# A pipelined four-layer graph network kernel: products with their high parts first, loop waits one group ahead, a new beginning and end

## The chip, the cores and the metric

One core of one Trainium2 chip. The metric is the device time of one execution in microseconds. The core's engines are TensorE (PE, matmuls and transposes), VectorE (DVE), ScalarE (ACT), GpSimd (POOL) and the queue of SyncE (SP), which issues every DMA.

## The reference

128 graphs of 128 nodes, 256 features each. x goes through four layers, each followed by a residual and a layer norm; adj is a sparse weighted 128x128 matrix per graph. Cut to what is computed (norm is a layer norm without gain, H = (adj != 0)):

```
h  = layernorm(relu(D^-1 H B^-1 H^T (x W1^T) + b1)) * gamma + beta     # 512 features
x1 = norm(2 x + D^-1 H B^-1 H^T (h W2^T) + b2)                          # layer 0
x2 = norm(x1 + relu([x1, adj x1 / rowsum(adj)] W^T))                    # layer 1
x3 = norm(x2 + adj(relu(adj(relu(adj(x2 V1)+b1) V2)+b2) V3)+b3)         # layer 2
x4 = norm(x3 + relu((adj x3) Wk) * any(x3 != 0))                        # layer 3
```

## The kernel before, in words

**The unit of work is a pair of graphs** (g = 0, 1); there are 64 pairs. Each pair passes through a chain of stages on TensorE, named in the code: G (the matrix of H B^-1 H^T), Tr (its transpose, after VectorE scaled it into Gd), Gx (G times the input), R (times W1), P (times W2) with squares (the sums for the layer norm of h), GP (G times P), xT (transpose of x1), XAB, AXB (layer 1), Ax2, H1, H1W, H2, H2W, AP3 (layer 2), Ax3, TK (layer 3). Between two stages ScalarE and VectorE, or GpSimd, take the result out of a bank of PSUM.

**fp32 by parts.** A product of two full-precision matrices is made of three passes in fp32r: each operand is held as a high part (rounded by a ScalarE copy, `high_...` or `round_...`) and a low part (the difference, `low_...` on VectorE or GpSimd); the passes are high x high, high x low, low x high. `product` (lines 377 to 382) issues the three of each term together. Before it, a stage waits for the high part and the low part of what it multiplies. Stages named propagate_T (Gx, Ax2, H2, Ax3) and the transposes (Tr, xT) use plain fp32 operands: eight 128x128 products, or two or four transposes.

**A software pipeline written out by hand.** Every engine has its own list of calls: `fill()`, then `body(n)` for n = 7 to 61 (FIRST to LAST - 1), then `drain()`. body(n) works on pairs n+1 to n-5 at once: G, Tr and Gx of pair n, R, P and GP of n-1, XAB and AXB of n-2, Ax2 to H2 of n-3, H2W to TK of n-4, norm n4 of n-5. The order within a queue is the order of the calls; queues meet only in semaphores (wait_ge). fill and drain are orders of their own, over 100 calls on most engines. The eight PSUM banks are given by BANK in the loop and by BANK_OF for stages in fill and drain. Because a bank is used again by another stage, TensorE's lists also have bare waits such as `pe.wait_ge(gt_hi, n)`: the reader of the old contents must be done. They may stand several calls ahead of the stage that writes the bank.

**The loop around the change.** On TensorE (lines 735 to 774) the order is R, G, xT, H2W, Ax2, XAB, H1, AP3, P, squares, Tr, AXB, H1W, Ax3, Gx, H2, GP, TK. Tr waits for gd_made (VectorE's Gd), Gx for gt_made (ScalarE's copy_GT of Tr's result) and for the input. On ScalarE (lines 1335 to 1370) square_mean waits for squares, VectorE turns its result into h_veps (wide_var), root_h takes the square root, make_x3 applies norm n3 (two activations of line 961, the second signals n3.done, for which Ax3 waits), then come round_p, copy_GT, copy_h1w, high_ax3, round_GT, high_gx. On GpSimd (lines 2199 to 2216) make_xb is followed by low_p (needs round_p), low_GT (needs round_GT), make_x2c, low_h2. SP reloads the inputs (a ring of four pairs) and stores x4.

Of the kernel before, what the change touches and what calls it, by code (L numbers as in the profile page):

```python
# [16 lines left out]
BANK = dict(R0=1, R1=0, Ax2=0, Tr=0, GP=4, H1=1, Gx=1, XAB=2, AXB=2, TK=2, H2=3, xT=4, P=4,  # L17
# [30 lines left out]
def build(nc, x, adjT, w1T, w2T, wab, v1, v2, v3, wk, columns, rows, eye, out):  # L48
    NP, C, GP_, D = x.shape
# [4 lines left out]
    with ExitStack() as ctx:  # L54
# [316 lines left out]
        def _(pe):  # L371
# [51 lines left out]
            def R(p, h):  # L423
                if p == 0:
                    pe.wait_ge(w1_lo, h + 1)
# [7 lines left out]
            def P(p, h):  # L433
                if p == 0 and h == 0:
                    pe.wait_ge(w2c_lo, 1)
# [1863 lines left out]
```

## Time and profile before

| | us |
|---|---|
| three runs | 1405.39, 1405.96, 1407.59 (median 1405.96) |
| the profiled execution, its own time | 1406.28 |
| its span in the profile | 1404.5 |
| TensorE matmul busy | 1378.7 (98%), 10896 instructions |
| TensorE weight loads busy | 1336.8 (95%) |
| VectorE, ScalarE, GpSimd busy | 1135.4 (81%), 1126.3 (80%), 1013.2 (72%) |
| DMA | 47.17 MB, mean 34 GB/s |

How to read it: matmuls are pipelined, each record of a matmul (0.28 us for 256 columns) overlaps its neighbours, which start about 0.12 us apart. So a hole of less than about 0.15 us between two starts doesn't show as idle time, and one looks at the starts. On ScalarE and VectorE, too, the next instruction starts before the record of the last one ends.

### The profile page before, as it was taken

How to read it: one execution, taken by the hardware profiler on the slowest of the kernel's cores; microseconds unless marked ns; L12 is line 12 of the kernel's file. 1: busy time of each engine (PE TensorE's matmuls, PEld its weight loads, DVE VectorE, ACT ScalarE, POOL GpSimd, SP SyncE). 2: the span in 40 equal slices, each digit the busy share in tenths (PEclk: the TensorE clock that was granted, in tenths of full speed). 3: DMA queues.
4: the chain of work that ended last, by engine and by line, in shares of the span. 5: the costliest groups of instructions: out<-in, count | busy, mean ns of one | idle time of the engine just before them, and what ended most of it. 6: DMA issues, size and time to landing. Idle time of an engine off the chain costs nothing. (4 is left out here: it accounts for less than half of the span.)

```text
span 1404.5 us, 35429 instructions
## 1 busy us (share of the span) xinstructions
PE 1378.7 (98%) x10896; PEld 1336.8 (95%) x10896; DVE 1135.4 (81%) x4086; ACT 1126.3 (80%) x2639; POOL 1013.2 (72%) x1065
## 2 busy tenths in 40 slices
PE   7999999999999999999999999999999999999995
PEld 7999999999999999999999999999999999999995
DVE  7888888787887887787887888877878877878886
ACT  6777887887887878878878878778878788788775
POOL 5857778777777787787787787777777877877530
PEclk9999999999999999999999999999999999999998
DMA  4100110101101101101101101011011011010001
GB/s 141 35 21 20 39 36 24 39 30 30 39 20 39 39 21 39 39 20 39 39 20 39 38 21 39 28 32 39 20 39 39 20 39 39 20 39 28 1 16 38
DMA packets 29961, 47.17 MB, mean 34 GB/s; under 512 B 3408, under 2 KB 12240, under 8 KB 29776
## 3 DMA queue, kind: packets, MB, share of 16 engines
q1 hardware_dynamic: 29776, 44.91, 10.1%
q8 instruction: 90, 1.47, 0.4%
q14 instruction: 95, 0.78, 0.2%
HBM read 28.12 MB, written 16.78 MB: 32 GB/s over the span
## 5 line engine op out<-in xcount | busy, mean ns | idle before, releaser
L961 ACT ACTIVATE x<-n_s,n_shift,n_rstd 128x256 f32<-128x256 f32 x384 | 208.4, 591 | 6.5 <-DVE n_shift L1550 5.1
L216 POOL TENSOR_TENSOR r_lo<-r_f,r_hi 128x512 fp32r<-128x512 f32 x122 | 157.7, 1293 | 45.3 <-ACT r_hi L942 40.1
L209 POOL TENSOR_TENSOR h_lo<-h_f,h_hi 128x512 fp32r<-128x512 f32 x122 | 158.1, 1296 | 40.3 <-ACT h_hi L942 40.1
L2111 POOL TENSOR_TENSOR n_s<-tk,mask 128x512 f32<-128x512 f32 x60 | 62.5, 1042 | 141.8 <-DVE mask L1603 135.1
L375 PE MATMUL psum<-v_hi,h_hi 128*128 128x256 f32 x512 | 149.6, 292 | 1.2 <-ACT tk L1123 1.0
L375 PE MATMUL psum<-w2c_hi,r_hi 128*128 128x258 f32 x512 | 145.8, 285 | 0.2 <-issue 0.2
L375 PE MATMUL psum<-w2c_lo,r_hi 128*128 128x258 f32 x512 | 144.5, 282 | 0.0
L375 PE MATMUL psum<-v_hi,h_lo 128*128 128x256 f32 x512 | 144.4, 282 | 0.0
L375 PE MATMUL psum<-gx_hi,w1T_hi 128*128 128x256 f32 x512 | 144.3, 282 | 0.1
L375 PE MATMUL psum<-v_lo,h_hi 128*128 128x256 f32 x512 | 144.1, 282 | 0.0
L1526 DVE BATCH_NORM_STATS2 n_st<-n_s 128x6 f32<-128x256 f32 x384 | 142.1, 412 | 2.2
L375 PE MATMUL psum<-gx_lo,w1T_hi 128*128 128x256 f32 x512 | 143.8, 281 | 0.0
L375 PE MATMUL psum<-gx_hi,w1T_lo 128*128 128x256 f32 x512 | 143.8, 281 | 0.0
L375 PE MATMUL psum<-w2c_hi,r_lo 128*128 128x258 f32 x512 | 143.8, 281 | 0.0
L375 PE MATMUL psum<-A_f,x 128*128 128x128 f32 x1024 | 136.2, 276 | 6.5 <-ACT x L961 6.1
L966 ACT ACTIVATE h_f<-psum,columns 128x256 f32<-128x256 f32 x256 | 107.6, 471 | 34.9 <-PE psum L375 34.6
L375 PEld LDWEIGHTS psum<-A_f,x 128*128 128x128 f32 x1024 | 125.5, 192 | 7.9 <-issue 7.8
L956 ACT ACTIVATE n_std<-psum,eps_c 128x2 f32<-128x2 f32 x165 | 42.3, 257 | 93.6 <-DVE psum L1535 93.6
L209 POOL TENSOR_TENSOR p_lo<-p_f,p_hi 128x512 fp32r<-128x512 f32 x61 | 78.1, 1280 | 51.5 <-ACT p_hi L942 51.5
L209 DVE TENSOR_TENSOR ax_lo<-psum,ax_hi 128x512 fp32r<-128x512 f32 x128 | 88.4, 691 | 26.8 <-ACT ax_hi L942 23.3
L375 PE MATMUL psum<-wab_hi,x1T_hi 128*128 128x512 f32 x256 | 106.5, 416 | 0.0
L966 ACT ACTIVATE r_f<-psum,columns 128x256 f32<-128x256 f32 x256 | 100.5, 468 | 2.2 <-PE psum L375 2.1
(166 smaller groups left out, 5379.8 us busy)
## 6 DMA issues: line engine op xcount, KB each, us to landing
x_in<-x_in_dram SPq DMA_DIRECT2D x64, 256.0 KB, 2.8
out<-x SPq DMA_DIRECT2D x64, 256.0 KB, 2.0
at_in<-adjT SPq DMA_DIRECT2D x64, 128.0 KB, 2.2
x<-v_in SPq DMA_DIRECT2D x3, 256.0 KB, 5.6
n_s<-w2T_in SPq DMA_DIRECT2D x2, 256.0 KB, 3.5
r_f<-w1T_in SPq DMA_DIRECT2D x2, 256.0 KB, 5.5
h_f<-wab_in SPq DMA_DIRECT2D x2, 256.0 KB, 5.9
tk<-wk_in SPq DMA_DIRECT2D x1, 256.0 KB, 5.5
```

Source lines behind the costliest of these rows:

```text
L209: return e.tensor_tensor(dst[1][:], src, f(dst[0][:]), ALU.subtract).then_inc(signal, 1)
L216: e.tensor_tensor(r_s[1][:, half], r_f[:, half], f(r_s[0][:, half]), ALU.subtract).then_inc(r_lo[h], 1)
L375: return pe.matmul(o, a, b, start=start, stop=stop)
L956: act.activation(nm.std[:], nm.mv(p)[:, :, 1], ACT.Sqrt, bias=eps_c[:, 0:1]).then_inc(nm.rooted, 1)
L961: last = act.activation(dst[:, g, :], nm.s[:, g, :], ACT.Identity, scale=nm.rstd[:, g:g + 1], bias=nm.shift[:, g:g + 1])
L966: return act.activation(dst[:, m].rearrange("p g c -> p (g c)"), psum[:, bank(stage, p), (m % 2) * 2 * C:(m % 2 + 1) * 2 * C], ACT.Relu, b ...
L1526: last = dve.bn_stats(nm.st[:, g, :], sum_in_psum(p, g) if nm is n1 else nm.s[:, g, :])
L2111: pool.tensor_tensor(n4.s[:], tk[:], bc(mask[:], [C, 2, D], 2), ALU.mult).then_inc(tk_masked, 1)
```

## The change

1. `product` is replaced by `early` (for each term high x high and the pass that takes the high part of the operand that comes last from the other engines, called state) and `late` (the pass with its low part). R, GP, H1, H1W, H2W, AP3 and TK issue early of the first half, wait for the low part, then late of it, then early and late of the second half; XAB, P and AXB issue early of both halves, wait, then late of both. Before early only the high part is waited for.
2. In the loop: on TensorE the waits of Tr (gd_made) and the bank wait ax2_lo stand ahead of squares; those of Gx (gt_made, x_loaded) with the two bank waits that stood between Ax3 and Gx ahead of Ax3; a wait for gx_lo stands ahead of R(n-1,0), the one for h2_relu ahead of R(n-1,1), the one for gt_hi ahead of H2. H2 writes bank 0 and not 3. ScalarE calls copy_GT ahead of root_h and round_GT ahead of make_x3. GpSimd calls low_GT ahead of low_p.
3. fill() and drain() of all engines have another order, with other engines for some of the low parts and sums, and another BANK_OF.
4. Each norm has a pad of its own for the memset ahead of bn_aggr.

The helpers and two of the stages (R stands for GP, H1, H1W, H2W, AP3 and TK; P for XAB and AXB):

```diff
-            def product(o, terms, start=True, stop=True):
-                for t, (a, b) in enumerate(terms):
+            def early(o, terms, state, start=True):
+                for t, ab in enumerate(terms):
+                    a, b = ab
                     mm(o, a[0], b[0], start and t == 0, False)
-                    mm(o, a[0], b[1], False, False)
-                    last = mm(o, a[1], b[0], False, stop and t == len(terms) - 1)
+                    mm(o, a[1 - state], b[state], False, False)
+
+            def late(o, terms, state, stop=True):
+                for t, ab in enumerate(terms):
+                    a, b = ab
+                    last = mm(o, a[state], b[1 - state], False, stop and t == len(terms) - 1)
                 return last
...
             def R(p, h):
...
                 pe.wait_ge(gx_hi, upto(p))
-                pe.wait_ge(gx_lo, upto(p))
...
+                for j, (o, terms) in enumerate(outs):
+                    early(o, terms, 0)
+                    if j == 0:
+                        pe.wait_ge(gx_lo, upto(p))
+                    last = late(o, terms, 0)
                 last.then_inc(pe_did[f"R{h}"], 1)
...
             def P(p, h):
...
+                pe.wait_ge(r_hi[h], upto(p))
+                for o, terms in outs:
+                    early(o, terms, 1, start=h == 0)
                 pe.wait_ge(r_lo[h], upto(p))
...
+                for o, terms in outs:
+                    late(o, terms, 1, stop=h == 1)
```

TensorE's loop:

```diff
             def body(n):
+                pe.wait_ge(gx_lo, n)
                 R(n - 1, 0)
-                pe.wait_ge(gt_hi, n)
+                pe.wait_ge(h2_relu, n - 3)
                 R(n - 1, 1)
...
                 pe.wait_ge(tk_relu, n - 4)
-                pe.wait_ge(h2_relu, n - 3)
                 XAB(n - 2)
...
                 P(n - 1, 0)
                 P(n - 1, 1)
+                pe.wait_ge(ax2_lo, n - 2)
+                pe.wait_ge(gd_made, upto(n))
                 squares(n - 1)
-                pe.wait_ge(ax2_lo, n - 2)
-                Tr(n)
+                Tr(n, waited=True)
                 AXB(n - 2)
                 pe.wait_ge(h2w_lo, n - 3)
                 H1W(n - 3)
-                Ax3(n - 4)
                 pe.wait_ge(h1_relu, n - 2)
                 pe.wait_ge(n4.shifted, n - 4)
-                Gx(n)
-                pe.wait_ge(n2.summed, n - 1)
+                pe.wait_ge(gt_made, upto(n))
+                pe.wait_ge(x_loaded[n % RING], inputs(n))
+                Ax3(n - 4)
+                Gx(n, waited=True)
+                pe.wait_ge(gt_hi, n + 1)
                 H2(n - 3)
```

ScalarE's and GpSimd's loop:

```diff
                 square_mean(n - 1)
+                copy_GT(n)
                 root_h(n - 1)
+                round_GT(n)
                 make_x3(n - 4)
                 round_p(n - 1)
-                copy_GT(n)
                 copy_h1w(n - 3)
                 high_ax3(n - 4)
-                round_GT(n)
                 high_gx(n)
...
                 make_xb(pool, n - 1)
+                low_GT(n)
                 low_p(pool, n - 1)
-                low_GT(n)
                 make_x2c(n - 3)
```

The beginning, cut to SP's loads (256 KB each, but 128 KB for at, 64 for the identity and 8 for the columns). Besides them, ScalarE's list now begins round_weights(0), round_inverse(0), copy_A(0), round_w1(0), round_weights(1), round_inverse(1), copy_GT(0) and has round_w1(1) four calls later (before: copy_A(0), round_weights(0), round_inverse(0), round_w1(0), round_inverse(1), round_weights(1), round_w1(1), copy_A(1), copy_GT(0)); GpSimd's begins split_weights(0), spread_high(0), spread_low(0) (before: spread_high(0), split_weights(0), spread_low(0)).

```diff
                 sp.dma_start(columns_s[:], columns).then_inc(columns_loaded, 16)
+                load_w2(1)
                 load_at(1)
-                load_w2(1)
                 load_w2(0)
+                sp.dma_start(ident[:], eye).then_inc(eye_loaded, 16)
+                load_w1(0)
                 load_at(2)
-                load_w1(0)
+                load_v(1)
                 load_x(0)
+                load_wab(0)
+                load_at(3)
+                load_w1(1)
                 load_v(2)
-                load_w1(1)
-                sp.dma_start(ident[:], eye).then_inc(eye_loaded, 16)
+                load_wab(1)
                 load_v(0)
...
```

The end. TensorE's drain before began with the waits for h1w_out, n2.shifted and p_made, then G(62), R(61,0), R(61,1), H2W(58); now R(61,0) is first, then come those for h1w_out and n2.shifted, G(62), H2W(58), R(61,1). Its last stages were AXB(63), H1(62), Ax3(60), H2W(61), H1W(62), Ax2(63), H2(62), AP3(61), TK(60), H1(63), H2W(62), Ax3(61), H1W(63), AP3(62), H2(63), TK(61), H2W(63), Ax3(62), AP3(63), TK(62), Ax3(63), TK(63). They are now AXB(63), Ax3(60), Ax2(62), AP3(61), H1(62), TK(60), H1W(62), Ax2(63), H2(62), Ax3(61), H1(63), H2W(62), TK(61), H1W(63), AP3(62), H2(63), H2W(63), Ax3(62), AP3(63), TK(62), Ax3(63), TK(63). sum_n4 of pairs 60 and 61 is called on GpSimd, of 58 on VectorE (before: the other way round), and low_h1(61) and low_h2(59) are now VectorE's.

## Rows read from the trace of the kernel before

**Rows 1.** Stretch, length, busy us of PE, PEld, DVE, ACT, POOL; PEclk, DMA share, GB/s.

```profile
0.00:124.00 124.00, 114.39 (x854) 107.70 (x855) 101.68 (x337) 89.20 (x213) 80.43 (x96) 1.00 0.18 58
124.00:1281.00 1157.00, 1156.89 (x9220) 1126.44 (x9219) 936.19 (x3414) 948.96 (x2226) 883.88 (x922) 1.00 0.11 33
1281.00:1404.50 123.50, 107.42 (x826) 102.64 (x824) 97.54 (x337) 88.10 (x202) 48.91 (x48) 0.95 0.05 18
```

**Rows 2.** The same view, of two stretches of the end.

```profile
1360.00:1380.00 20.00, 18.40 (x150) 17.60 (x149) 17.92 (x62) 16.70 (x37) 4.73 (x4) 1.00 0.04 15
1390.00:1404.50 14.50, 4.62 (x20) 4.09 (x20) 4.67 (x21) 5.19 (x11) 0.00 (x0) 0.56 0.10 36
```

**Rows 3.** Timeline of TensorE, one pass of the loop: start, us, instruction, [idle before].

```profile
700.33 0.60 PE L461 MATMUL psum<-ident,x 128*128 128x128 f32 x4
700.68 0.37 PE L375 MATMUL psum<-v_hi,h_hi 128*128 128x256 f32 x1
...
702.20 1.06 PE L375 MATMUL psum<-A_f,x 128*128 128x128 f32 x8
...
711.29 0.41 PE L415 MATMUL psum<-ident,Gd 128*128 128x128 f32 x2
711.46 0.36 PE L375 MATMUL psum<-xbw_hi,A_hi 128*128 128x258 f32 x1
...
713.70 1.05 PE L375 MATMUL psum<-A_f,x 128*128 128x128 f32 x8
714.59 1.10 PE L375 MATMUL psum<-GT,x_in 128*128 128x128 f32 x8
715.53 1.06 PE L375 MATMUL psum<-A_f,h1w 128*128 128x128 f32 x8
...
721.72 0.49 PE L461 MATMUL psum<-ident,x 128*128 128x128 f32 x3
721.97 0.37 PE L375 MATMUL psum<-v_hi,h_hi 128*128 128x256 f32 x1
```

**Rows 4.** Timeline of ScalarE in the same pass.

```profile
712.06 0.20 ACT L1046 ACTIVATE h_std<-h_veps 128x2 f32<-128x2 f32 x1 [0.43 <-DVE h_veps L1653]
712.21 1.09 ACT L961 ACTIVATE x<-n_s,n_shift,n_rstd 128x256 f32<-128x256 f32 x2
...
713.95 0.36 ACT L942 ACTIVATE GT<-psum 128x256 f32<-128x256 f32 x1
714.21 0.59 ACT L942 ACTIVATE h1w<-psum 128x512 f32<-128x512 f32 x1
```

**Rows 5.** Timeline of ScalarE, from the beginning of the kernel.

```profile
25.87 0.20 ACT L1046 ACTIVATE h_std<-h_veps 128x2 f32<-128x2 f32 x1
25.98 0.62 ACT L942 ACTIVATE r_hi<-r_f 128x512 fp32r<-128x512 f32 x1
```

**Rows 6.** Timeline of TensorE, end of the kernel.

```profile
1295.28 0.48 PE L375 MATMUL psum<-BH,HT 128*128 128x258 f32 x2 [0.83 <-issue]
...
1391.30 1.72 PE L375 MATMUL psum<-A_f,x 128*128 128x128 f32 x8 [3.23 <-ACT x L961]
1394.52 0.55 PE L375 MATMUL psum<-wk_hi,ax_hi 128*128 128x256 f32 x1 [1.50 <-DVE ax_lo L209]
```

**Rows 7.** Timeline of ScalarE, end of the kernel.

```profile
1390.06 1.09 ACT L961 ACTIVATE x<-n_s,n_shift,n_rstd 128x256 f32<-128x256 f32 x2 [0.87 <-DVE n_shift L1550]
1393.05 0.60 ACT L942 ACTIVATE ax_hi<-psum 128x512 fp32r<-128x512 f32 x1 [1.90 <-PE psum L375]
```

**Rows 8.** Timeline of TensorE, beginning of the kernel.

```profile
6.14 0.80 PE L375 MATMUL psum<-BH,HT 128*128 128x258 f32 x2 [6.14 <-POOL BH L2089]
...
116.32 0.91 PE L375 MATMUL psum<-A_f,x 128*128 128x128 f32 x6 [1.24 <-ACT x L961]
```

**Rows 9.** Timeline of GpSimd in the pass of rows 3.

```profile
714.12 1.28 POOL L209 TENSOR_TENSOR p_lo<-p_f,p_hi 128x512 fp32r<-128x512 f32 x1 [0.46 <-ACT p_hi L942]
715.80 0.73 POOL L209 TENSOR_TENSOR GT_lo<-GT,GT_hi 128x256 fp32r<-128x256 f32 x1 [0.40 <-issue]
```

More of the change, by code:

```diff
@@ L448, in GP @@
             def GP(p):
+                outs = [(psum[:, bank("GP", p), g * D:(g + 1) * D],
+                         [(part(GT_s[p % 2], ALL, g), part(p_s, ALL, g))]) for g in range(2)]
                 pe.wait_ge(p_hi, upto(p))
-                pe.wait_ge(p_lo, upto(p))
                 pe.wait_ge(gt_lo, upto(p))
-                for g in range(2):
-                    last = product(psum[:, bank("GP", p), g * D:(g + 1) * D],
-                                   [(part(GT_s[p % 2], ALL, g), part(p_s, ALL, g))])
+                for j, (o, terms) in enumerate(outs):
+                    early(o, terms, 0)
+                    if j == 0:
+                        pe.wait_ge(p_lo, upto(p))
+                    last = late(o, terms, 0)
                 last.then_inc(pe_did["GP"], 1)
@@ L490, in H1 @@
             def H1(p):
[L491 to L492 removed]
                 if p == 0:
                     pe.wait_ge(v_lo, 1)
[L495 to L497 removed]
+                outs = [(psum[:, bank("H1", p), m * 2 * C:(m + 1) * 2 * C],
+                         [(part(v_s[0], ALL, kk, cols(m)), part(ax2, ALL, kk)) for kk in range(KD)])
+                        for m in range(KD)]
+                pe.wait_ge(ax2_hi, upto(p))
+                for j, (o, terms) in enumerate(outs):
+                    early(o, terms, 0)
+                    if j == 0:
+                        pe.wait_ge(ax2_lo, upto(p))
+                    last = late(o, terms, 0)
                 last.then_inc(pe_did["H1"], 1)
@@ L502, in H1W @@
                     pe.wait_ge(v_lo, 2)
+                outs = by_state("H1W", p, h1_s, v_s[1])
                 pe.wait_ge(h1_hi, upto(p))
-                pe.wait_ge(h1_lo, upto(p))
-                weigh("H1W", p, h1_s, v_s[1])
+                for j, (o, terms) in enumerate(outs):
+                    early(o, terms, 1)
+                    if j == 0:
+                        pe.wait_ge(h1_lo, upto(p))
+                    last = late(o, terms, 1)
+                last.then_inc(pe_did["H1W"], 1)
             def H2(p):
@@ L650, in fill @@
                 XAB(2)
-                pe.wait_ge(h2_relu, 1)
-                H2W(0)
-                pe.wait_ge(h1_relu, 2)
+                pe.wait_ge(r_relu[1], 5)
+                AP3(0)
+                pe.wait_ge(h2w_lo, 1)
                 H1W(1)
@@ L728, in fill @@
                 Gx(6)
-                pe.wait_ge(n2.summed, 5)
+                pe.wait_ge(gt_hi, 7)
                 H2(3)
@@ L856, in drain @@
-                pe.wait_ge(n3.summed, 60)
-                AXB(61)
-                pe.wait_ge(n1.done, 63)
                 TK(58)
                 pe.wait_ge(xbw_lo, 62)
-                H2(60)
+                P(63, 0)
+                pe.wait_ge(n3.summed, 60)
+                H1W(60)
+                P(63, 1)
+                pe.wait_ge(h1_relu, 61)
+                H2(60)
+                pe.wait_ge(tk_relu, 59)
+                Ax2(61)
+                pe.wait_ge(n2.summed, 62)
+                Ax3(59)
@@ L1240, in fill @@
+                high_gx(4)
+                copy_h1w(0)
+                root(n2, 1)
+                round_GT(4)
+                square_mean(3)
+                make_x2(1)
+                relu_h2(0)
+                root_h(3)
+                round_h2(0)
+                root(n1, 2)
+                round_p(3)
                 relu_r(4, 0)
-                relu_h1(0)
-                round_GT(4)
-                round_h1(0)
+                high_x1T(2)
+                high_ax2(1)
                 relu_r(4, 1)
-                root(n2, 1)
@@ L1433, in drain @@
-                root_h(63)
+                relu_h1(60)
+                round_h1(60)
+                make_x4(57)
+                relu_tk(58)
+                round_r(63, 1)
+                copy_A(62)
+                root(n1, 62)
+                root(n2, 61)
+                root(n3, 59)
                 copy_h1w(60)
-                round_p(63)
-                high_x1T(62)
-                relu_tk(58)
+                make_x2(61)
+                make_x3(59)
                 relu_h2(60)
```

1168 lines of the change are left out of this document (609 added, 559 removed), and 39 rows, old and new, of the table BANK_OF.

## The prediction

> **What bounds the kernel now.** I read the busy time by stretch first. TensorE is the bound: it idles 9.61 us of the first 124 (6.14 of them ahead of its first product [rows 8], 3.47 after), 0.11 of the 1157 us of the loop, and 16.08 of the last 123.5; VectorE is at 81% in the loop, and nearly saturated (17.92 of 20) in the stretch from 1360 [rows 1, 2]. So time can come out of the loop only where TensorE's own stream has holes too small to count as idle. They show in the starts of one pass of the loop [rows 3]. A pass is 21.29 us (700.68 to 721.97). Eight plain fp32 products with more of their kind behind take 0.89 us (Ax3, 713.70 to 714.59), but Gx, eight of the same size with H2 behind, takes 0.94 (to 715.53): a hole of 0.05. xT's four transposes take 0.35 and its last three 0.25 (721.72 to 721.97), so one takes 0.10 to 0.11, and Tr, two of them, should cost 0.35 - 0.21 = 0.14; Tr takes 0.17: 0.03. Nothing else in a pass is open to this change.
>
> **The loop, part by part.** There are 55 passes (7 to 61). (a) Gx's hole is a late release: ScalarE has written GT at 714.31 (713.95 + 0.36), and Gx begins 0.28 later, at 714.59 [rows 3, 4]. The change puts the copy of GT ahead of root_h, at about 711.7 where Tr ends, so GT is there 2 us before it is needed, and Gx follows Ax3 without a wait of its own: -0.05 a pass, -2.8 us. (b) The waits for Tr move ahead of squares, all on things long done: at best -0.03 a pass, -1.7 us; at worst nothing, if the 0.03 is the price of switching to transposes. (c) What pays: round_GT now stands between root_h and make_x3. On ScalarE root_h begins 712.06 and make_x3 712.21, and x3 is written at 713.30 (1.09 later); Ax3 begins at 713.70, so there are 0.40 us between [rows 3, 4]. A copy of GT's size lets the next one start after 0.26 (713.95 to 714.21) [rows 4]; a square root of this size lets a copy start after 0.11 [rows 5]. The new order is 0.11 + 0.27 in place of 0.15: x3 comes 0.23 later, and 0.17 are left. The first GT copy costs root_h nothing: it can begin at Tr's end, 711.7, frees the engine at about 712.0, and root_h waits for VectorE until 712.06 anyway. How much must be between? Where x3 is the only thing missing and two waits stand ahead of the group, it is 0.15 (x of pair 63 is written at 1391.15, Ax3 begins 1391.30) [rows 6, 7]. Where four waits are gathered ahead of a group it was 0.28 (Gx, above). The change gathers five ahead of Ax3: h1_relu, n4.shifted, gt_made, x_loaded and n3.done. So Ax3 is between 0.02 too early and 0.11 too late; I take 0.05 late, just under the middle of the two. That eats all of (a). It eats (b) too: x3's chain starts at squares, ahead of Tr, so a faster Tr only reaches Ax3's wait sooner. Everything behind Ax3 (Gx, H2, GP, TK, the next pass) follows it unchanged. **Loop: 0.0 us, between -4.4 (neither is eaten) and +3.3** (0.06 a pass).
>
> The Trainium skill weighs in here on both sides. Perfetto Trace Analysis, section Identifying Dependency Chains, says that an instruction that waits for several engines may get EventSemaphore instructions ahead of it for the further conditions. By that rule x3's wait turns from one on the weight load into one of its own; the 0.28 against 0.15 agrees. TensorE: Matmul & The Clock Gate, section Architectural detail, gives TensorE a queue of 64 in which weight loads are pulled ahead; by that alone earlier waits would free the loads, and the loop would give the whole -4.4.
>
> (d) The passes within a product change order: all with the high part first, then a wait for the low part on the rest. Their number does not change. In the loop no product waits for a low part (0.11 us idle), so 0. Should a wait inside a product hold up the next load, 12 such waits a pass at 0 to 0.03 (Tr's hole, the nearest row to such a price) would cost 0 to 0.36 a pass. H2W, which begins behind four waits, needs 1.52 for its 12 passes with the switch from xT in them, 0.12 and a bit each, with no such hole [rows 3]; so I take 0; the upper end, +20 us, gets a chance of 0.02, outside the range. (e) H2 goes from bank 3 to bank 0, behind gt_hi, which at 712.06 + 0.11 + 0.36 = 712.5 is early enough for 715.5. On GpSimd low_GT now runs ahead of low_p: 0.73 us of work, 0.46 of it in the time in which low_p was waited for [rows 9], so p_lo ends 0.27 later, at 715.67. GP stands behind H2's eight products (from 715.53, some 0.8 us) and needs p_lo only for its third pass: 0. A later x3 also pushes copy_h1w and the next ScalarE work by under 0.1, as the copy of GT that stood there is gone: 0. (f) The separate pads of the memsets: 0. SP's order in the loop is unchanged.
>
> **The beginning.** The same work in another order of all queues, SP's loads too. 3.47 us can be had after the first product; the largest piece is 1.24 us, Ax3(2) waiting for x [rows 8]. I see two gains worked out of the order: split_weights(0) leaves the way of the first product (about 0.15), and copy_GT(0) is no longer behind copy_A(1) and the round of w1's second half, which lets Gx(0) start some 0.3 earlier. w1's second half lands later (448 KB more are ahead of it) but is needed only by R(0,1). Of the rest, low parts that arrive late are now hidden under up to four passes (0.47). I take -1.3, bounds -3.5 and +1.2 (another wait like the 1.24).
>
> **The end.** (1) G(62) stood 0.83 idle [rows 6] on n2.shifted; now R(61,0), 12 passes, is ahead of that wait: -0.8. (2) From H1(63) on, one chain sets the end. A product starts now 0.15 after the high part and not after the low part. TK(63) has its high part at 1393.65 and starts at 1394.52, 0.87 later [rows 6, 7]; 0.72 of that can go, as far as passes are there to fill it. TK has four, at half the clock 0.24 each: 0.7. H2W(63) has four at 0.12: 0.5. AP3(63) has two: 0.2. Sum 1.4; H1 and H1W of pair 63 may give as much again, but VectorE, 90% busy there [rows 2], takes that back in part: 0.4. (3) sum_n4 of pairs 60 and 61 goes from VectorE to GpSimd, 0.7 us each, partly on the way: 0.4. Together **-3.0**, bounds 0 and -5.5 (all of it, and H1's). Nothing changes behind the last TK.
>
> **Sum** against the profiled execution: 1406.28 (its span is 1404.5), 0.32 above the median shown, 1405.96. -1.3 + 0.0 - 3.0 = -4.3: **1402.0 us**.
>
> **The rivals.** About 0.2% (2.8 us) is what can be told from no change.
> A. *The waits give all they can.* Ax3 is not late: 0.08 a pass, -4.4, and 1397.6. For it: 0.15 was enough where x3 alone was missing. Against it: five waits in a row. Chance 0.16.
> B. *x3 late in full, slower.* round_GT costs ScalarE the whole 0.36 of such a copy [rows 4] and not 0.23, and TensorE needs the 0.28: Ax3 is 0.24 late, net of Gx's hole 0.19 a pass, +10.5, and 1412.5. It makes the kernel slower by over 0.2% once Ax3 is later than 0.18. Against it: copies overlap by 0.1 in every row. Chance 0.09.
> C. *The new ends bring nothing*, because the hand-written order leaves its waits elsewhere: where a chain of latencies sets the end, a queue that runs 1 us late shows at once. 1406.3. Chance 0.21.
> D. *The clock holds.* From 1390 the granted clock is 0.56 [rows 2], mostly 1.2 GHz: Ax3(63) takes 1.72 us against 1.05 [rows 3, 6], and TK(63)'s 12 passes of 0.12 take twice their 1.4. If less idling ahead of them keeps 2.4 GHz, 2.1 us more go: 1399.9. Against it: the 3.23 us of waiting for x3(63) stay. Chance 0.08. By the Trainium skill (TensorE: Matmul & The Clock Gate, What's actually happening) the clock follows how busy TensorE has been; that speaks for the drop staying, as that idling does.
> My forecast has the remaining 0.44 (0.02 are the waits inside the products, under d), with its own spread of 1399.5 to 1404.5.
>
> **Numbers.** Faster: A, D and 0.36 of the forecast, 0.60. Same: C and 0.06 of the forecast, 0.27. Slower: B, the 0.02 of (d) and 0.02 of the forecast, 0.13. The range 1397.4 to 1407.0 takes in A, C and D, leaves out B, (d) and the outer ends of the bounds.
>
> **What would show it.** Right: in the profile after, Gx has no hole and Ax3's start is up to 0.1 later behind H1W, a pass is 21.25 to 21.33 us, x3 is written 0.23 later after root_h; G(62) without its 0.83; TK(63) beginning about 0.15 to 0.3 after ax_hi. Wrong in the loop: a pass of 21.21 (A) or above 21.45 (B). Wrong at the ends: TensorE idle for 16 us or more in the last 123 as before, or for more than 9.6 in the first 124.

## The result, and the profile after

The changed kernel takes **1395.71 us** (median of four runs: three lie between 1395.13 and 1396.00, and the fourth took 1678.93 at a mean granted clock of 0.751, where the others had 0.996) beside 1405.68 for the kernel before: the ratio is 0.9925, with a 95% interval of 0.9905 to 0.9944. The prediction had 1402.0, and its range began at 1397.4: the direction was right, the size was not, and the time lies below the range. The profiled execution took 1395.13 us, 11.15 less than the profiled 1406.28 of before; its span is 1393.0, 11.5 less.

Busy time by stretch of the kernel after (columns as in [rows 1]; the last two lines answer to [rows 2], moved with the end):

```profile
0.00:124.00 124.00, 116.14 (x883) 111.08 (x884) 103.46 (x348) 91.74 (x220) 76.83 (x93) 1.00 0.20 61
124.00:1281.00 1157.00, 1156.76 (x9267) 1125.47 (x9266) 944.69 (x3440) 948.54 (x2236) 885.21 (x932) 1.00 0.10 32
1281.00:1393.00 112.00, 98.44 (x751) 93.68 (x749) 86.62 (x306) 81.40 (x184) 39.57 (x36) 0.95 0.06 20
...
1360.00:1380.00 20.00, 15.03 (x120) 14.10 (x118) 14.34 (x54) 14.87 (x35) 2.51 (x2) 0.98 0.08 27
1380.00:1393.00 13.00, 4.95 (x20) 4.42 (x20) 3.79 (x16) 4.14 (x10) 0.00 (x0) 0.63 0.11 42
```

The counts beside the busy times say more than the busy times: in the same 1157 us TensorE executed 9267 passes where it executed 9220, busy for 1156.8 and 1156.9 us. The loop got faster without any idle time being taken out of it. In the first 124 us 29 more passes fit in, and TensorE idles 7.86 us where it idled 9.61.

The starts of G(7) and G(61), the first and the last G of the loop, part the kernel into beginning, loop and end. Timeline of TensorE, the kernel before and then the kernel after:

```profile
124.24 0.40 PE L375 MATMUL psum<-BH,HT 128*128 128x258 f32 x2
...
1275.82 0.40 PE L375 MATMUL psum<-BH,HT 128*128 128x258 f32 x2
```

```profile
120.86 0.40 PE L374 MATMUL psum<-BH,HT 128*128 128x258 f32 x2
...
1266.55 0.40 PE L374 MATMUL psum<-BH,HT 128*128 128x258 f32 x2
```

Beginning: 124.24 to 120.86, -3.4 us. Loop between the two: 1151.58 to 1145.69, -5.9. From G(61) to the end of the span: 128.7 to 126.45, -2.2. Sum -11.5.

One pass of the loop in the kernel after, first TensorE, then ScalarE (to be laid beside [rows 3, 4]):

```profile
704.87 0.42 PE L418 MATMUL psum<-ident,Gd 128*128 128x128 f32 x2
705.04 0.36 PE L374 MATMUL psum<-xbw_hi,A_hi 128*128 128x258 f32 x1
...
707.27 1.10 PE L374 MATMUL psum<-A_f,x 128*128 128x128 f32 x8
708.21 1.06 PE L374 MATMUL psum<-GT,x_in 128*128 128x128 f32 x8
709.10 1.06 PE L374 MATMUL psum<-A_f,h1w 128*128 128x128 f32 x8
...
712.12 0.28 PE L374 MATMUL psum<-gx_hi,w1T_hi 128*128 128x256 f32 x1
...
714.86 0.40 PE L374 MATMUL psum<-BH,HT 128*128 128x258 f32 x2
```

```profile
705.32 0.38 ACT L988 ACTIVATE GT<-psum 128x256 f32<-128x256 f32 x1
705.64 0.20 ACT L1092 ACTIVATE h_std<-h_veps 128x2 f32<-128x2 f32 x1
705.75 0.37 ACT L988 ACTIVATE GT_hi<-psum 128x256 fp32r<-128x256 f32 x1
706.01 1.08 ACT L1007 ACTIVATE x<-n_s,n_shift,n_rstd 128x256 f32<-128x256 f32 x2
```

Gx now takes 0.89 (708.21 to 709.10) and not 0.94; Ax3, ahead of it, takes 0.94 (707.27 to 708.21) and not 0.89. make_x3 begins 0.37 after root_h (705.64 to 706.01), 0.22 later than before, and x3 is there at 707.09, 0.18 ahead of Ax3. So the terms (a) and (c) came at the sizes that were written, and cancel; how Ax3's 0.05 arises is taken up below. Tr still takes 0.17. And yet a pass is 21.180 us where it was 21.307 (medians of the starts of G, taken to the nanosecond; all times of a group with three decimals below are such medians over the 50 or more full passes, from the start of a group's first pass to the start of the next group's, in one profiled execution of each kernel). The group that changed is the last one, R with its 24 passes ("pass" is used both for one turn of the loop and for one matmul; a product has 6, 12 or 24 of the second kind): 712.12 to 714.86, 2.731 us where it took 2.837. That is 0.106 of the 0.127. H2W gives 0.016, AXB 0.013, H1 0.010, XAB 0.006; P costs 0.029 more.

### The profile page after: what moved, and what is told of

The parts are those of the page before. It is cut to its first block, busy times and chain, and to the rows that moved or that the text cites. A ratio compares the mean times of both kernels' runs of the same rounds, so it can differ in the third digit from the quotient of the medians.

```text
span 1393.0 us, 35235 instructions
## 1 busy us (share of the span) xinstructions
PE 1371.3 (98%) x10896; PEld 1330.2 (95%) x10896; DVE 1134.8 (81%) x4092; ACT 1121.7 (81%) x2639; POOL 1001.6 (72%) x1059
## 4 chain that ended last, share of the span: by engine, by line
PE 98%; ACT 1%; issue 0%; DVE 0%; DMA 0%; SPq 0%; ACTq 0%; DVEq 0%
PE psum L374 94%; PE psum L475 2%; PE psum L418 1%; DMA n_s<-w2T_in 0%; ACT x L1007 0%; ACT tk L1169 0%; ACT h_hi L988 0%; DVE w2c_lo L1782 0%; ACT ax_hi L988 0%; ACT w2c_hi L988 0%; DVE w2g L1764 0%; ACT r_f L1012 0%; SPq L291 0%; ACT h_f L1012 0%; DVE n_st L1572 0%
## 5 line engine op out<-in xcount | busy, mean ns | idle before, releaser
L374 PE MATMUL psum<-v_hi,h_hi 128*128 128x256 f32 x512 | 138.1, 292 | 2.0 <-ACT h_hi L988 2.0
L374 PE MATMUL psum<-v_lo,h_hi 128*128 128x256 f32 x512 | 133.6, 282 | 0.0
L374 PE MATMUL psum<-w2c_hi,r_hi 128*128 128x258 f32 x512 | 129.6, 285 | 0.9 <-DVE w2c_lo L1782 0.9
L374 PE MATMUL psum<-gx_hi,w1T_hi 128*128 128x256 f32 x512 | 130.3, 279 | 0.0
L374 PE MATMUL psum<-gx_hi,w1T_lo 128*128 128x256 f32 x512 | 129.6, 278 | 0.0
L374 PE MATMUL psum<-w2c_lo,r_hi 128*128 128x258 f32 x512 | 129.4, 283 | 0.0
L374 PE MATMUL psum<-v_hi,h_lo 128*128 128x256 f32 x512 | 102.0, 281 | 0.0
L374 PE MATMUL psum<-wab_lo,x1T_hi 128*128 128x512 f32 x256 | 100.9, 394 | 0.0
L208 DVE TENSOR_TENSOR x1T_lo<-psum,x1T_hi 128x512 fp32r<-128x512 f32 x64 | 44.2, 691 | 69.0 <-ACT x1T_hi L988 69.0
L374 PE MATMUL psum<-gx_lo,w1T_hi 128*128 128x256 f32 x512 | 100.3, 277 | 0.0
```

Source lines behind the costliest of these rows:

```text
L208: return e.tensor_tensor(dst[1][:], src, f(dst[0][:]), ALU.subtract).then_inc(signal, 1)
L374: return pe.matmul(o, a, b, start=start, stop=stop)
```

## The experiments

Three theories stood for R: the order of its passes; the places of its buffers, since the change takes `wait_pad` out ahead of x_in (each buffer takes a multiple of 32 bytes of every partition, so all from x_in to n1 lie 32 bytes lower); and the waits around it.

**The 32 bytes, put into the kernel before, and taken from the changed one.**

```diff
-        eps_c, wait_pad = sb("eps_c", [1]), sb("wait_pad", [1])
+        eps_c = sb("eps_c", [1])
...
+        wait_pad = sb("wait_pad", [1])
```

> The kernel before with one edit: the 4-byte buffer wait_pad is declared last in place of ahead of x_in, so every buffer from x_in to n4's lies 32 bytes lower, as it does in the changed kernel. Order theory (R's passes run at a better pace because of the order high x high, low weights x high, then high weights x low): R's 24 passes keep their 2.84 us and a pass of the loop its 21.31 us; the time is that of the kernel before, within 0.1%. Layout theory (the pace hangs on where the operands lie, moved by 32 bytes): R's 24 passes take 2.73 us, a pass of the loop about 21.20, the kernel 55 x 0.11 = 6 us less. Wait theory (the waits for gt_hi and h2_relu moved around R set the pace): no change, 21.31.

Measured: 1399.17 us, ratio to before 0.9953 (0.9939 to 0.9968). A pass 21.257.

```diff
-        eps_c = sb("eps_c", [1])
+        eps_c, shift_pad = sb("eps_c", [1]), sb("shift_pad", [1])
```

> The changed kernel with one edit: a 4-byte buffer stands again where wait_pad stood, so all buffers from x_in on lie 32 bytes higher, as in the kernel before. Order theory: R's passes keep 113.8 ns, a pass 21.18 us, 1395.7 us. Layout theory: R goes back to 118 ns a pass, a pass of the loop to about 21.29, the kernel to about 1402. Wait theory: no change, 21.18.

Measured: 1399.87 us, ratio 0.9956 (0.9942 to 0.9971). A pass 21.284, R 2.833.

**The order of R's passes, put into the kernel before, and taken from the changed one.** The edit is shown with the passes of `product` written out; the other run is its inverse, with both of R's waits ahead of its first pass.

```diff
                     for t, (a, b) in enumerate(terms):
                         mm(o, a[0], b[0], t == 0, False)
-                        mm(o, a[0], b[1], False, False)
-                        last = mm(o, a[1], b[0], False, t == KD - 1)
+                        mm(o, a[1], b[0], False, False)
+                    for t, (a, b) in enumerate(terms):
+                        last = mm(o, a[0], b[1], False, t == KD - 1)
```

> The kernel before with only R's passes in the new order (per output: high x high and low weights x high for both terms, then high weights x low), both of R's waits still ahead of its first pass. Order theory: R's 24 passes 2.73 us, a pass of the loop 21.20, the kernel 6 us less than before. Layout theory and wait theory: R keeps 2.84 us, a pass 21.31, the time of before.

Measured: 1405.81 us, ratio 1.000 (0.999 to 1.001). R 2.838, a pass 21.307.

> The changed kernel with only R's passes in the old order (high x high, high weights x low, low weights x high for each term) and both waits ahead of R's first pass. Order theory: R goes back to 118 ns a pass, 2.84 us, a pass of the loop to 21.29, the kernel to about 1401.5. Layout theory and wait theory: R keeps 113.8 ns, a pass 21.18, the kernel 1395.7.

Measured: 1396.88 us, ratio 0.9938 (0.9923 to 0.9953). R 2.823 in the median, a pass 21.271.

What follows: the order of R's passes alone is worth nothing (on the kernel before, to 0.1%), the 32 bytes are worth some 4 us on the changed kernel and 6.6 us on the kernel before. But neither theory explains the run with the old order in the new places, where R lost its pace again. Taken pass by pass, R has **two values and none between** in the new places: 2.731 and 2.823 us. The fast one came in 47 of the 55 passes of the changed kernel, in 27 of 55 in the kernel before with the 32 bytes, in 16 of 55 with R's old order, and in none of the kernel before or of any run with the old places, whose R takes 2.833 to 2.845. So the waits of the new loop do not bring it by themselves either: the changed kernel with the old places has them all. All passes in the loop of the changed kernel, the run with the old places, by group (line, engine, names, shapes, count, busy us, mean ns of one, idle):

```profile
L374 PE MATMUL psum<-gx_hi,w1T_hi 128*128 128x256 f32 x432 | 109.3, 277 | 0.0
L374 PE MATMUL psum<-gx_hi,w1T_lo 128*128 128x256 f32 x432 | 109.3, 277 | 0.0
L374 PE MATMUL psum<-gx_lo,w1T_hi 128*128 128x256 f32 x432 | 84.6, 277 | 0.0
```

```profile
L374 PE MATMUL psum<-gx_lo,w1T_hi 128*128 128x256 f32 x432 | 86.2, 281 | 0.0
```

The record of one pass is 4 ns shorter in the mean; from start to start it is 113.8 ns (2.731 / 24) for 118.0 (2.833 / 24).

**Which places?** Two simple rules were tried on the changed kernel.

```diff
+        pad_w = sb("pad_w", [16])
         wab_s, wk_s = hi_lo("wab", [KD, 2 * D]), hi_lo("wk", [KD, D])
         v_s = [hi_lo(f"v{j}", [KD, D]) for j in range(3)]
...
+        pad_c = sb("pad_c", [16])
         columns_s, rows_b = sb("columns", [3 * KH + 2 * KD]), sb("rows", [2, D])
```

> The changed kernel with the weights wab, wk and v1 to v3 64 bytes higher (a 64-byte pad ahead of them and one behind, so that all else lies as before modulo 128): every weight then begins at a multiple of 128 bytes, as w1 does. The gain of the 32-byte shift showed in R above all, and there only with the new order of passes, which reads the same moving operand twice in a row. Theory of the pair (R is fast since its weights begin at 0 modulo 128 and its moving operand at 64): H1, the same shape and order as R, falls from 118 to 114 ns a pass, 12 passes from 1.42 to 1.37 us, a pass of the loop from 21.18 to about 21.13. Theory of the line (only whether an operand begins at a multiple of 64 bytes counts, and all of these do already): H1 1.42, a pass of the loop 21.18 as before.

```diff
+        pad_x = sb("pad_x", [16])
         x_in = sb("x_in", [RING, 2, D])
```

> The changed kernel with a 64-byte pad ahead of x_in: all buffers but the weights lie 64 bytes higher, gx at 0 modulo 128 like w1. Theory of the pair: R loses its pace and goes back to 2.82 us for 24 passes, a pass of the loop 21.27. Theory of the line: R stays at 2.73 us, a pass of the loop 21.18.

```diff
-        ... hi_lo("w2c", [KH, D + 2])
+        ... hi_lo("w2c", [KH, D + 16])
-        ... hi_lo("xbw", [2, D + 2])
+        ... hi_lo("xbw", [2, D + 16])
```

> The changed kernel with the rows of w2c and xbw 272 elements long (1088 bytes, 17 times 64) where they had 258 (1032 bytes), the products reading 258 of them as before; pads keep all other buffers where they were modulo 128. P's moving operand then begins at a multiple of 64 bytes in every pass, where it begins 8, 16 and 24 bytes off, and w2c_lo 32 bytes off. Theory of the line: P's 24 passes go from 2.90 us to 24 x 115 ns = 2.76, AXB's six from 0.81 to 0.79, a pass of the loop to about 21.03, the kernel some 8 us less than the changed one. Theory of the pair and of the order: P keeps its weights in turn and stays at 2.90, a pass of the loop 21.18.

Measured: weights 64 bytes higher 1398.71 us (0.9953; 0.9937 to 0.9969), H1 1.416, R 2.821 in every pass, a pass 21.280. States 64 bytes higher 1396.55 (0.9937; 0.9917 to 0.9956), R 2.856 in every pass, but XAB 2.858 for 2.884, P 2.857 for 2.902, H2W 1.496 for 1.507, H1W 1.413 for 1.423; TK 1.430 for 1.415; a pass 21.240. Rows of 1088 bytes 1397.67 (0.9945; 0.9925 to 0.9964), P 2.900, R fast in 11 of 55, a pass 21.267. (Only AXB, whose rows were changed with P's, went as the rule of the multiples had it, from 0.807 to 0.792.) Both rules fall: H1 with the remainders of R did not get R's pace, R did not keep its own at multiples of 64, and P with every row at a multiple of 64 bytes gained 0.002. What stands is that moving buffers moves the time of a product by 0.01 to 0.045 us. It need not be the product's own operands that move: with the weights of other products 64 bytes higher, R lost its fast value and P rose to 2.914, though the operands of both kept their remainders by 128.

**The late x3.** The term (c) of the prediction, undone:

```diff
                 root_h(n - 1)
-                round_GT(n)
                 make_x3(n - 4)
+                round_GT(n)
```

> The changed kernel with one ScalarE step of the loop moved: round_GT stands behind make_x3 and no longer ahead of it. Theory of the prediction (c): x3 comes 0.23 us earlier, Ax3's 0.05 goes (0.941 to 0.89 us), Gx stays at 0.893, a pass of the loop 21.18 to 21.13, the kernel 2.8 us less. Rival: H2, behind gt_hi, or p_hi behind round_GT becomes late, and the pass stays at 21.18 or more.

Measured: 1395.66 us, ratio 0.9926 (0.9909 to 0.9942): the time of the changed kernel. Ax3 went from 0.941 to 0.888, as (c) has it. But R went to 2.823 in 54 of 55 passes, 0.092 each, though only ScalarE's order had been touched; the pass is 21.213 for 21.180. The loop as a whole, G(7) to G(61), takes the same in both (1145.8 and 1145.7 us): Ax3 pays for most of R's loss, and eight passes of the changed kernel for the rest. In those eight x3 is written 0.06 to 0.31 us later than in the others, and Ax3 begins 0.04 to 0.29 later behind H1W, 0.9 us in all; with x3 earlier this is 0.1. Which rhythm R will have can be read 2 us ahead of it, in the starts of GP's passes. With the old order of R, where both occur, GP's second pass is 0.112 to 0.117 us long in the fast cases and mostly 0.116 in the slow ones, and its fourth 0.122 to 0.124 against 0.112 to 0.120: the rhythm is there when TensorE leaves H2, and stays through GP, TK and R. In the changed kernel the eight passes with a slow R are just the eight in which Ax3 began late.

**Does the instant at which GP begins select it?** First waits, then work ahead of GP, each on the run with round_GT moved:

```diff
                 pe.wait_ge(p_made, n)
+                pe.wait_ge(ax2_lo, n - 2)
+                pe.wait_ge(h1_relu, n - 2)
+                pe.wait_ge(n4.shifted, n - 4)
+                pe.wait_ge(r_relu[0], n)
                 GP(n - 1)
```

> The run with round_GT behind make_x3, and in the loop four more waits ahead of GP, all on things long done. In the runs so far R's 24 passes took one of two times, 2.731 or 2.823 us: the first in 47 of 55 passes of the changed kernel, in 17 of 55 with R's old order, in 27 of 55 with the layout alone, in 1 with round_GT moved, in none of the kernel before; which of the two showed already in the starts of GP's passes, some nanoseconds apart, 2.2 us ahead of R. Rhythm theory (the pace is set by the instant at which TensorE starts again, to a few ns, and is then kept): waits that move GP's start can turn R from 2.823 to 2.731 in all passes, and the loop by 0.09 a pass, though nothing of R, its operands or their place has changed. Rival (R's pace hangs on its own operands and order): R stays at 2.823.

(The 17 of 55 in this text is a miscount for 16.) Measured: 1394.43 us (0.9922; 0.9902 to 0.9941). Inconclusive: the four waits moved nothing, GP takes 0.784 with and without them, R is fast in 2 of 55. It shows that waits on things long done are free for TensorE here.

```diff
                 pe.wait_ge(gt_lo, upto(p))
+                if 7 <= p < 61:
+                    mm(psum[:, bank("GP", p), 0:16], GT_s[p % 2][0][:, 0, :], p_s[0][:, 0, 0:16], True, True)
```

> The run with round_GT behind make_x3 (a pass of the loop 21.213 us, R always 2.823), and in the loop one extra pass of 16 columns ahead of GP's first, into the same bank, overwritten by it. Rhythm theory: the extra pass costs 0.03 to 0.06 us (the one-column passes of squares take 0.028 to 0.112 each) and moves the start of GP, TK and R against what sets the pace; R then takes 2.731 in many passes, and a pass of the loop is 21.213 + 0.05 - 0.09 = 21.17. Rival (R's pace comes with Ax3's wait for x3 itself, or with R's own operands): R stays at 2.823, a pass of the loop 21.25.

> As the run with the short pass, with 64 columns in place of 16: the same theories, another shift. By the rhythm theory at least one of the two shows R at 2.731 in passes of the loop; if both stay at 2.823 throughout, a shift of GP's start alone does not select it, and the theory falls in that form.

Measured: with 16 columns 1401.85 us (0.9973; 0.9963 to 0.9984), with 64 columns 1397.06 us (0.994; 0.992 to 0.996). Timeline of TensorE in one pass of the loop, GP's start with the short pass in the same row, its second pass, TK's start, R's start and G behind R; 16 columns first, then 64:

```profile
713.12 0.48 PE L374 MATMUL psum<-p_hi,GT_hi 128*128 128x16 f32 x2
713.43 0.28 PE L374 MATMUL psum<-p_hi,GT_lo 128*128 128x256 f32 x1
...
714.03 0.28 PE L374 MATMUL psum<-wk_hi,ax_hi 128*128 128x256 f32 x1
...
715.44 0.28 PE L374 MATMUL psum<-gx_hi,w1T_hi 128*128 128x256 f32 x1
...
718.26 0.40 PE L374 MATMUL psum<-BH,HT 128*128 128x258 f32 x2
```

```profile
710.07 0.48 PE L374 MATMUL psum<-p_hi,GT_hi 128*128 128x64 f32 x2
710.38 0.28 PE L374 MATMUL psum<-p_hi,GT_lo 128*128 128x256 f32 x1
...
710.98 0.28 PE L374 MATMUL psum<-wk_hi,ax_hi 128*128 128x256 f32 x1
...
712.39 0.28 PE L374 MATMUL psum<-gx_hi,w1T_hi 128*128 128x256 f32 x1
...
715.12 0.40 PE L374 MATMUL psum<-BH,HT 128*128 128x258 f32 x2
```

GP and TK take the same to 0.01 us (0.91 and 1.41) in both; R takes 2.82 in one (715.44 to 718.26) and 2.73 in the other (712.39 to 715.12). It is so throughout: 52 of 53 passes slow with 16 columns, 53 of 53 fast with 64, and the pass of the loop is 21.340 and 21.240. This is the clean pair of the study: the two kernels differ in the width of one pass, 2.3 us ahead of R, and in nothing of R. That what stands ahead of GP's passes selects the rhythm is shown; by what it is kept is not. The short pass costs 0.12 us (GP 0.91 for 0.784; 0.03 to 0.06 had been expected), more than R gives back.

**The ends alone.** The changed kernel with the loop bodies of the kernel before on three engines, H2 in bank 3 and the old places. The new order of the passes within a product stays in it:

```diff
-TK=2, H2=0,
+TK=2, H2=3,
...
             def body(n):
+                pe.wait_ge(gx_lo, n)
                 R(n - 1, 0)
+                pe.wait_ge(gt_hi, n)
                 R(n - 1, 1)
...
```

> Only the new beginning and end: the changed kernel with the bodies of the loop on TensorE, ScalarE and GpSimd as in the kernel before, H2 of the loop in bank 3, and the buffers from x_in on 32 bytes higher as before. If the ends give what the two traces show for them (the loop entered 3.4 us sooner, the rest from G(61) on 2.2 us shorter), the kernel takes some 5.5 us less than the one before, about 1400.4, with passes of 21.29 to 21.31 us. The prediction had 4.3 for them. Rival: half of the gain at the ends is layout too, and the kernel takes only 3 us less.

Measured: 1400.69 us, ratio 0.9965 (0.9952 to 0.9978); its span is 1398.5. Timeline of TensorE, G(7) and G(61):

```profile
120.10 0.40 PE L374 MATMUL psum<-BH,HT 128*128 128x258 f32 x2
...
1270.92 0.40 PE L374 MATMUL psum<-BH,HT 128*128 128x258 f32 x2
```

Beginning -4.1, loop -0.8, from G(61) on -1.1 (127.6 for 128.7): 6.0 of span. The kernel with the new loop but the old places has the same span, 1398.5, and a pass of 21.284 for 21.290. **So in the old places the edits to the loop bodies are worth nothing that can be told, the ends are worth 6.0 of span, and the places of the buffers the remaining 5.5**, 4.8 of them in the loop. These are single profiled executions, and that of the old places was the longest of its four; by the ratios to the kernel before (0.9965, 0.9956, 0.9925) the ends are worth 4.9 us, the loop bodies 1.3, with overlapping intervals, and the places 4.4. In the new places the loop bodies may be worth something: the old loop there had R fast in 27 passes, the new one in 47. No run parts this from the change of the fast passes from execution to execution that is shown below.

**Putting the gains together.** Three runs, in the order of the texts: P's old order in the loop on the changed kernel; round_GT moved and states 64 bytes higher; round_GT moved and P's old order.

> The changed kernel with P's passes of the loop in the old order, both waits ahead. P took 2.873 us before, 2.880 with the layout alone and 2.902 in the changed kernel. If the order costs P this, it goes back to 2.88 and a pass of the loop to 21.16; R's 2.73 may be kept or lost (2.82), as P ends 0.02 us sooner: by the rhythm theory Ax3 waits for x3 all the same, and R keeps 2.73 in most passes.

> Both edits together: round_GT behind make_x3, and all buffers from x_in on 64 bytes higher. Alone, the first took Ax3's wait away (0.941 to 0.888 us) and lost R's fast rhythm; the second made XAB, P, H2W and H1W 0.026, 0.045, 0.011 and 0.010 us shorter and R 0.03 longer than its slow value. If these add, a pass of the loop is 21.240 less 0.067 = 21.17 us and the kernel as fast as the changed one (1395.7), with no rhythm needed; if they don't, it is 21.21 or more, about 1397.5.

> The changed kernel with round_GT behind make_x3 and P's passes of the loop in the old order. One took 0.053 us a pass from Ax3 and gave 0.092 back in R; the other took 0.022 from P with R's 2.731 kept. If nothing makes TensorE wait, R goes at 2.823 as with the first edit alone: a pass of the loop 21.213 - 0.022 = 21.19 us, and the kernel about 1395. If P's earlier end happens to bring the fast rhythm, 21.10 and about 1390.

Measured: P's old order 1393.33 us in one round (0.9914; 0.9894 to 0.9934), P 2.880 for 2.902, a pass 21.160, R fast in 49 of 55. Round_GT with the states higher 1395.66 (0.9927; 0.9911 to 0.9944), a pass 21.213 and not 21.17: Ax3's wait went, but R rose to 2.870 and TK to 1.447, so the gains did not add. Both small gains 1394.23 (0.9921; 0.9904 to 0.9937), a pass 21.193, R slow in 53 of 55, as expected where nothing makes TensorE wait.

Last, only the buffers from r to x3 were moved, with gx (R) left in place and ax3 (TK) 128 bytes higher, at the same remainder by 128. The three runs are this with both small gains, this with P's old order alone, and P's old order again without it:

```diff
+        pad_r = sb("pad_r", [16])
         r_f, r_s = sb("r_f", [KH, 2, C]), hi_lo("r", [KH, 2, C])
...
+        pad_3 = sb("pad_3", [16])
         ax3 = hi_lo("ax3", [KD, 2, C])
```

> The run with both small gains (a pass 21.193 us, R 2.823), and all buffers from r to x3 64 bytes higher, gx and ax3 left where they are. Where all states were moved by 64 bytes, XAB fell from 2.884 to 2.858, P from 2.902 to 2.857, H2W from 1.507 to 1.496, H1W from 1.423 to 1.413, while R (moving operand gx) rose to 2.856 and TK (stationary operand ax3) to 1.430. If each product's time hangs on where its own two operands lie, the four gains stay and the two losses do not come: 0.026 + 0.045 + 0.011 + 0.010 = 0.09 a pass, 21.10 us, the kernel about 1389.3. Rival: the gains hang on the whole arrangement or on the moments at which the products begin, and the pass stays at 21.19 or more.

> The changed kernel with P's old order, and the same shift of the buffers from r to x3. Own-operand theory: a pass of 21.160 - 0.09 = 21.07 us if R keeps the 2.731 that Ax3's wait gave it, 21.16 if the shift of the other products' ends loses it (2.823): R's share of fast passes tells.

> The changed kernel with P's old order, as run before in one round (1393.33 us, a pass 21.160 us against 21.180). Expected again 1393.3 to 1394.3 us, the gain of P (0.022 a pass) kept: below the changed kernel's 1395.7 by 0.1 to 0.2%.

Measured: **1387.06 us**, ratio to the kernel before 0.9871 (0.9856 to 0.9886), for both small gains in the split places: 8.7 us below the changed kernel, and the best of the study. With Ax3's wait left in 1390.63 (0.9894; 0.9880 to 0.9907), a pass 21.147, R fast (2.746 here) in 26 of 55; but TK takes 1.42 in the passes with the fast R and 1.38 in the others, so that the fast rhythm gives back only 0.04 a pass there. P's old order again 1395.58 (0.9927; 0.9915 to 0.9940), which is the time of the changed kernel and outside the 1393.3 to 1394.3 expected: R was fast in 30 of 55 passes, in the same kernel that had 49 before. So the fast rhythm of the changed kernel is not a property of the kernel alone. The two runs were on different chips, so whether the chip or the execution decides is open. Timelines of TensorE in a pass with the small gains in the old arrangement and in the split one (TK, R, G; then XAB, H1; then P, squares):

```profile
709.30 0.28 PE L374 MATMUL psum<-wk_hi,ax_hi 128*128 128x256 f32 x1
710.72 0.28 PE L374 MATMUL psum<-gx_hi,w1T_hi 128*128 128x256 f32 x1
713.54 0.41 PE L374 MATMUL psum<-BH,HT 128*128 128x258 f32 x2
...
716.45 0.48 PE L374 MATMUL psum<-wab_hi,x1T_hi 128*128 128x512 f32 x1
719.34 0.28 PE L374 MATMUL psum<-ax_hi,v_hi 128*128 128x256 f32 x1
...
721.47 0.28 PE L374 MATMUL psum<-w2c_hi,r_hi 128*128 128x258 f32 x1
724.35 0.50 PE L374 MATMUL psum<-ones,sq 128*128 128x1 f32 x4
```

```profile
706.23 0.29 PE L376 MATMUL psum<-wk_hi,ax_hi 128*128 128x256 f32 x1
707.61 0.28 PE L376 MATMUL psum<-gx_hi,w1T_hi 128*128 128x256 f32 x1
710.44 0.41 PE L376 MATMUL psum<-BH,HT 128*128 128x258 f32 x2
...
713.34 0.48 PE L376 MATMUL psum<-wab_hi,x1T_hi 128*128 128x512 f32 x1
716.20 0.28 PE L376 MATMUL psum<-ax_hi,v_hi 128*128 128x256 f32 x1
...
718.33 0.28 PE L376 MATMUL psum<-w2c_hi,r_hi 128*128 128x258 f32 x1
721.18 0.50 PE L376 MATMUL psum<-ones,sq 128*128 128x1 f32 x4
```

TK falls from 1.42 to 1.38, XAB from 2.89 to 2.86, P from 2.88 to 2.85, R stays at 2.82 to 2.83; with H1W (1.424 to 1.408) and H2W (1.506 to 1.497) a pass is 21.093 for 21.193. 0.09 of this was expected from XAB, P, H2W and H1W (they gave 0.08); TK's 0.034 was not, and neither of TK's operands had changed its remainder by 128; R, whose operands had not moved at all, went from 2.823 to 2.827. The idea that each product's time hangs on where its own two operands lie, by which the gain was forecast, is not shown by the gain. All 55 passes have R slow but two, so nothing here rests on the fast rhythm.

## Why the prediction was wrong

**The step that failed is (f), "The separate pads of the memsets: 0".** It was read as a change of what VectorE writes; it also takes a buffer out from ahead of all others. By the run with the pad put back that is -5.5 us of span (-4.4 by the ratios), of which R's rhythm is most: 47 passes by the 0.102 between 2.833 and 2.731, and 8 by 0.010, are 4.9. No row of before showed it: there every R took 2.833 or more. The row that could have warned is another: passes of equal shape whose starts scatter by 10 ns were taken for one constant, "0.12 and a bit".

**(d), the order of the passes: 0.** Right for R (ratio 1.000), and for P in the places from which it was read: with the old places P takes 2.869 in the new order and 2.873 in the old. In the new places it takes 2.902 and 2.880, so that there the new order costs 0.022 a pass of the loop, 1.2 us in all. The +20 us, with a chance of 0.02, did not come: R has such a wait among its passes and still runs them at 113.8 ns.

**(a), (b), (c): 0.0 in the loop.** Right in the sizes: Gx -0.048, Ax3 +0.051, Tr's 0.03 unchanged with its waits long past, x3 0.22 later (0.23 said), and undoing (c) gave the 0.053 back. How much must lie between x3 and Ax3 shows in the start of Ax3's second pass, for its first is not late (1.423 behind H1W's, for 1.426). In the kernel before x3 was the last thing missing in two passes of the loop, and there the second pass began 0.265 us after x3 was written. In the changed kernel, with five waits gathered ahead of Ax3, it begins 0.33 after, in all 55 passes. Less the 0.112 of a step, this is a lead of 0.15 that was needed before and of 0.22 now; 0.17 are there, and 0.05 are lost. So the 0.15 of the prediction was right, and gathered waits do raise it, by 0.06. The 0.22 is the middle that the prediction took between two rows, a guess that came out. The pass of 21.180 lay below even the 21.21 of rival A, whose mechanism did not happen: its time, 1397.6, was nearest for the wrong reason. Rival B (x3 late in full) did not happen as it was written; x3 was so late in eight of the 55 passes alone, for 0.9 us in all and not 10.5. The sign of a right prediction, a pass of 21.25 to 21.33, is met by the run with the old places: 21.284.

**(e), bank 0 and low_GT ahead of low_p: 0.** Right: GP takes 0.794 before and after.

**The beginning, -1.3, mis-sized.** It measures -4.1 with the ends alone, beyond the bound of -3.5, and -3.4 in the changed kernel. The waits of TensorE in the first 124 us, after:

```profile
PE psum L374 <- POOL BH L2204: 6.0, 1, 6.0
PE psum L374 <- DVE w2c_lo L1782: 0.9, 1, 0.9
PE psum L374 <- DVE w2g L1764: 0.9, 1, 0.9
```

split_weights gave its 0.15 (5.97 for 6.14). The wait of 1.24 for x in [rows 8], which the estimate left standing, is gone, and two waits on weights, one of which was there before, are all that is left. Idle time fell by 1.75; as both kernels execute the same 856 passes ahead of G(7), the rest came out of the steps from one pass's start to the next, which the profile does not count as idle. The estimate priced only what could be read out of the order by hand, and put nothing for these steps.

**The end, -3.0.** It measures -1.1 alone and -2.2 in the changed kernel. Its first part is right: G(62) stands without its 0.83. The chain is right in form and was eaten in size. End of the kernel after, TensorE, then ScalarE:

```profile
1286.37 0.40 PE L374 MATMUL psum<-BH,HT 128*128 128x258 f32 x2
...
1380.19 2.04 PE L374 MATMUL psum<-A_f,x 128*128 128x128 f32 x8 [3.22 <-ACT x L1007]
1383.02 0.55 PE L374 MATMUL psum<-wk_hi,ax_hi 128*128 128x256 f32 x1 [0.78 <-ACT ax_hi L988]
```

```profile
1382.28 0.60 ACT L988 ACTIVATE ax_hi<-psum 128x512 fp32r<-128x512 f32 x1 [2.04 <-PE psum L374]
```

The granted clock (last column but two) over Ax3(63), before and then after:

```profile
1391.20:1393.10 1.90, 1.72 (x8) 1.46 (x8) 0.00 (x0) 0.05 (x1) 0.00 (x0) 0.62 0.00 0
1380.10:1382.30 2.20, 2.04 (x8) 1.78 (x8) 0.99 (x6) 0.16 (x2) 0.00 (x0) 0.50 0.00 0
```

ax_hi is there at 1382.88 and TK(63) begins 0.14 later, for 0.87 before [rows 6, 7]: 0.7 as said. But Ax3(63) takes 2.04 us for 1.72, now with 0.50 of the clock (1.2 GHz) throughout, where 0.62 was granted before, so Ax3 to TK shrank by 0.39 only. And the idling moved ahead: from 1360 to 1380 TensorE is busy 15.03 of 20 us, where it was 18.40. The same low clock speaks against rival D. Beginning and end together, -4.3 said, are -4.9 by the run with the ends alone (0.35%, with an interval of 0.22 to 0.48), so rival C did not happen; but the sum is near only because the beginning gave more than was said and the end less.

## What to carry to other kernels

A kernel bound by back-to-back TensorE passes should have its buffers' places counted among its edits: a pad that moves everything by 32 or 64 bytes is worth as much here (0.3% to 0.5%) as the whole new beginning and end, and the arrangement can be searched with pads, one group of buffers at a time, read off group by group in the trace. When a change moves the time and no idle row explains it, compare the start-to-start time of each group of passes, and look whether a group has one value or several. An edit that wins by a rhythm can lose it with the next one, or in another execution of the same kernel.

## What the runs showed of the hardware

- R's 24 passes of 256 columns have two rhythms, 113.8 and 117.6 ns a pass, at a granted clock of 2.4 GHz in both; which one holds is settled ahead of GP's passes, 2 us sooner (a pass of 16 columns there: 52 of 53 slow; of 64: 53 of 53 fast), and is then kept through TK and R, 36 passes. The Trainium skill (TensorE: Matmul & The Clock Gate, Wait — 56ns, not 53.3ns?) gives back-to-back passes N / 2.4 GHz and about 2.5 ns; for 256 columns that is an estimate of 109.2 ns, and no fp32r product here reached it.
- The time of a product changes when buffers are moved: P 2.902 to 2.857 us, XAB 2.884 to 2.858 and TK 1.413 to 1.379 by moves of 64 bytes, R 2.837 to 2.823 or 2.731 by 32. P, TK and R changed also in runs in which their own operands kept their remainders by 128 (P 2.902 to 2.914, TK 1.413 to 1.379, R 2.823 to 2.827). Two rules (remainders by 128 of the pair, multiples of 64) were refuted; the right one stays open, as does what keeps the rhythm.
- Ax3, eight plain fp32 passes, has its second pass 0.265 us after its last operand is written with the old waits ahead of it, and 0.33 after with five waits gathered there; the loss shows only in the starts, and no idle time is counted for it.
- A pass of 16 or of 64 columns costs the stream 0.12 us, as much as one of 256 (GP 0.911 and 0.906 us with it, 0.784 without). Four more waits on things long done cost nothing where all of a group's waits are long past (a pass of the loop 21.213 us with and without them).
